# 16-wide attentions with another order of query halves, and a norm whose powers and products are split between GpSimd and VectorE

## The reference, cut to what matters

```python
Q = split_heads(x @ Wq.T)        # 16 heads, 16 wide
K = split_heads(x @ Wk.T)
V = split_heads(x @ Wv.T)
scores = jnp.einsum('bhqd,bhkd->bhqk', Q, K) / jnp.sqrt(jnp.float32(HEAD_DIM))
causal = jnp.tril(jnp.ones((s, s), dtype=bool))
scores = jnp.where(causal, scores, jnp.float32(-jnp.inf))
attn = jax.nn.softmax(scores, axis=-1)
```

```python
nrm = jnp.linalg.norm(x, axis=-1, keepdims=True) * d ** (-0.5)
h = norm_scale * x / (nrm + EPS) * split_scale      # EPS = 1e-08
```

## Time and profile before

| | |
|---|---|
| time, 3 runs | 3187.84, 3194.51, 3197.19 us; median 3194.51 us |
| the profiled execution | 3189.21 us; its span 3187.5 us |
| mean granted TensorE clock of the span | 0.983 |
| busy: TensorE, VectorE, ScalarE, GpSimd | 2986.1, 1373.9, 1113.0, 588.8 us |

### The profile page before, as it was taken

The page is one execution under the profiler, slowest core; times in us unless marked ns, Lnnn a source line. Parts: engine busy times, 40 slices in busy tenths (PEclk is TensorE's granted clock), DMA queues, the critical chain, the costliest instruction groups (busy, mean ns, idle before and its releaser), DMA issues. The chain is left out here.

```text
span 3187.5 us, 40136 instructions
## 1 busy us (share of the span) xinstructions
PE 2986.1 (94%) x15070; PEld 1793.0 (56%) x15070; DVE 1373.9 (43%) x3111; ACT 1113.0 (35%) x1988; POOL 588.8 (18%) x821
## 2 busy tenths in 40 slices
PE   7989999889999999999999999999999999989756
PEld 3443455644465555556666666656776778644413
DVE  6758424576144114212233333333333332277497
ACT  3635414446132113111433433323333332236432
POOL 2020012120002222222000000023333331120163
PEclk9999999999999999999999999999999999999989
DMA  3021000030102331322100000000000000120131
GB/s 84 27 58 50 25 23 26 7 72 6 48 11 76 88 101 44 89 84 81 42 11 10 14 12 22 1 31 12 15 16 11 16 32 12 37 62 22 59 125 60
DMA packets 70507, 129.25 MB, mean 41 GB/s; under 512 B 15918, under 2 KB 43920, under 8 KB 70048
## 3 DMA queue, kind: packets, MB, share of 16 engines
q1 hardware_dynamic: 68396, 125.12, 13.2%
q10 hardware_dynamic: 1920, 1.57, 0.4%
HBM read 99.55 MB, written 1.54 MB: 32 GB/s over the span
## 5 line engine op out<-in xcount | busy, mean ns | idle before, releaser
L186 POOL TENSOR_SCALAR shift<-mv 128x1 f32<-128x1 f32 (+1 forms) x98 | 21.8, 223 | 1465.9 <-DVE scale L171 1465.7
L2289 DVE TENSOR_TENSOR L1f_inner<-L1f_ps_up,L1f_gate 128x512 f32<-128x512 f32 x96 | 66.4, 691 | 362.3 <-PE L1f_ps_up L2188 362.2
L1537 ACT ACTIVATE L2b_tanh<-L2b_ps_scores,L2b_inverse 128x512 f32<-128x512 f32 x192 | 110.6, 579 | 303.4 <-PE L2b_ps_scores L1495 303.4
L2270 ACT ACTIVATE L1f_gate<-L1f_ps_gate 128x512 f32<-128x512 f32 x96 | 57.4, 597 | 399.7 <-PE L1f_ps_gate L2169 399.7
L1134 ACT ACTIVATE L0f_weights<-L0f_ps_scores 128x1024 f32<-128x1024 f32 (+1 forms) x192 | 149.8, 812 | 111.1 <-PE L0f_ps_scores L966 84.1
L2152 POOL TENSOR_TENSOR L1f_inner<-L1f_inner,L1f_weight 128x512 f32<-128x512 f32 x96 | 119.2, 1266 | 365.8 <-DMA L1f_weight<-combine 350.6
L1504 PEld LDWEIGHTS L2b_ps_out<-L2b_v,L2b_weights 128*128 128x128 f32 x1152 | 141.3, 193 | 33.7 <-issue 28.4
L1942 ACT ACTIVATE L2a_probs<-L2a_ps_scores,L2a_negmax 128x512 f32<-128x512 f32 (+7 forms) x128 | 95.1, 743 | 172.3 <-DVE L2a_negmax L1976 172.3
L1495 PE MATMUL L2b_ps_scores<-L2b_q,L2b_k 128*128 128x512 f32 (+3 forms) x384 | 147.4, 487 | 1.0 <-DVE L2b_q L1597 0.8
L1504 PE MATMUL L2b_ps_out<-L2b_v,L2b_weights 128*128 128x129 f32 x1152 | 143.7, 277 | 2.9 <-POOL L2b_weights L1413 2.8
L1839 PE MATMUL L2a_ps_scores<-L2a_k,L2a_q 128*128 128x512 f32 (+3 forms) x384 | 145.2, 487 | 0.0
(11 more groups left out here) (639 smaller groups left out, 6274.1 us busy)
## 6 DMA issues: line engine op xcount, KB each, us to landing
L1f_w<-in_L1f_w SPq DMA_DIRECT2D x32, 384.0 KB, 3.8
L1f_weight<-combine SPq DMA_DIRECT2D x32, 384.0 KB, 4.5
L1f_weight<-combine SPq DMA_DIRECT2D x32, 256.0 KB, 4.7
scan_spread_b<-bc SPq DMA_DIRECT2D x16, 512.0 KB, 4.5
scan_spread_c<-bc SPq DMA_DIRECT2D x16, 512.0 KB, 3.9
L0f_qs<-L0f_part SPq DMA_DIRECT2D x96, 64.0 KB, 2.6
experts_early<-in_L1f_w SPq DMA_DIRECT2D x16, 384.0 KB, 3.6
L2a_early<-in_L2a_w SPq DMA_DIRECT2D x16, 384.0 KB, 3.1
```

The source lines that it names most:

```text
L1537: nc.scalar.activation(tanhs[u % 3][:, at:], ps_scores[u % 3][:, at:], ACT.Tanh, scale=inverse[e][:, NT + kt:NT + kt + 1]).then_inc(capped, 1)
```

## The change

In the attentions the second unit is now (quad 1, half 0) in place of (quad 0, half 1), so units 0 and 1 are both of half 0. The start written by hand has p6, v1 and p7 in other places: p7 now stands ahead of t0. The transfers of the stacked queries and keys follow the new order of units. r0, r2, r3, y4, y6 and f0 stand at other slots. In the norm GpSimd keeps the two powers, and three VectorE operations (`find_shift`) make the sum with the product by 1e-8, the reciprocal, and the shift; the constant -1 for the third power is gone. The number of idle-filling matmuls ahead of each of the last three turns is 4 in place of 8.

```diff
-QUAD_UNITS = [(0, 0), (0, 1), (1, 1), (2, 1), (3, 1), (1, 0), (2, 0), (3, 0)]
+QUAD_UNITS = [(0, 0), (1, 0), (0, 1), (1, 1), (2, 1), (3, 1), (2, 0), (3, 0)]
...
-    order = ("p0 p1 p2 p3 v0 p4 m0 m1 m2 p5 m3 m4 m5 v1 m6 m7 m8 p6 m9 m10 v2 m11 m12 m13 t0 p7 "
+    order = ("p0 p1 p2 p3 v0 p4 m0 m1 m2 p5 m3 m4 m5 p6 m6 m7 m8 v1 m9 m10 p7 m11 v2 m12 m13 t0 "
              "m14 m15 m16 v3 m17 m18 m19").split()
...
-    then(3, 1, "r2")
-    then(5, 1, "r3")
-    then(6, 1, "r0")
+    then(2, 1, "r0")
+    then(4, 1, "r2")
+    then(6, 1, "r3")
     if factor:
-        then(6, 0, "f0")
+        then(7, 0, "f0")
     else:
-        then(6, 0, "y4")
-        then(7, 0, "y6")
+        then(7, 0, "y4")
+        then(7, 1, "y6")
...
-            stack(0, 1)
+            stack(1, 0)
             sp.dma_start(ks[SPLIT:WITH_MAX, :, :, :].rearrange("i a h t -> i (a h t)"), core.ones_rows
                          ).then_inc(ones_in, 16)
             for u in range(NU):
+                if u < 2:
+                    stack(u, 1)
+                elif u < QUADS:
+                    stack(u, 1)
+                    stack(u, 0)
                 place_max(u)
-                if u < QUADS - 1:
-                    stack(u + 1, 0)
-                    stack(u + 1, 1)
...
-        pool.wait_ge(done, n + 1)
-        pool.tensor_scalar(scale, scale, 1e-8, None, ALU.mult).then_inc(done, 1)
-        pool.wait_ge(done, n + 3)
-        pool.tensor_tensor(scale, scale, shift, ALU.add).then_inc(done, 1)
-        pool.wait_ge(done, n + 4)
-        pool.tensor_tensor(scale, scale, inverse, ALU.pow).then_inc(done, 1)
-        pool.wait_ge(done, n + 5)
-        pool.tensor_tensor(shift, mean, scale, ALU.mult).then_inc(self.turned_mean, 1)
-        pool.wait_ge(self.turned_mean, g + 1)
-        pool.tensor_scalar(shift, shift, -1.0, None, ALU.mult).then_inc(self.shifted, 1)
+
+    def find_shift(self, dve, g):
+
+        if self.kind != "norm":
+            return
+        core, part = self.core, self.tiles(g)
+        scale, shift = core.scale[:, part], core.shift[:, part]
+        dve.wait_ge(self.scaled, 2 * (g + 1))
+        dve.scalar_tensor_tensor(scale, scale, 1e-8, shift, ALU.mult, ALU.add).then_inc(self.inverted, 1)
+        dve.wait_ge(self.inverted, 2 * g + 1)
+        dve.reciprocal(scale, scale).then_inc(self.inverted, 1)
+        dve.wait_ge(self.inverted, 2 * g + 2)
+        dve.scalar_tensor_tensor(shift, core.mv[:, part, 0], -1.0, scale, ALU.mult, ALU.mult).then_inc(self.shifted, 1)
...
-                keep_busy(core, ps_out[0][:], 8 if following.kind == "norm" else 4)
+                keep_busy(core, ps_out[0][:], 4)
...
                 following.find_spread(nc.vector, t)
+                if t:
+                    following.find_shift(nc.vector, t - 1)
                 if t >= 4:
                     following.keep_dve(nc.vector, t - 4, free_bank(t - 4))
+            following.find_shift(nc.vector, NT - 1)
```

More of the change, by code:

```diff
@@ L41, in __init__ @@
         self.zeros = sb("zeros", [P, HALF], BF16)
-        self.powers = sb("powers", [P, 3 * NT])
+        self.powers = sb("powers", [P, 2 * NT])
         self.ident = sb("ident", [P, P])
@@ L120, in open @@
         self.x_added, self.measured, self.spread = st.sem("next_x_added"), st.sem("next_measured"), st.sem("next_spread")
-        self.scaled, self.turned_mean = st.sem("next_scaled"), st.sem("next_turned_mean")
+        self.scaled, self.inverted = st.sem("next_scaled"), st.sem("next_inverted")
         self.shifted, self.rows_act = st.sem("next_shifted"), st.sem("next_rows_act")
@@ L181, in find_scale @@
         size = part.stop - part.start
-        inverse_root, root, inverse = (core.powers[:, n * NT:n * NT + size] for n in range(3))
-        n = (5 if self.kind == "norm" else 2) * g
+        inverse_root, root = (core.powers[:, n * NT:n * NT + size] for n in range(2))
+        n = 2 * g
         if self.kind != "norm":
@@ L306, in _ @@
             nc.vector.memset(core.powers[:, NT:2 * NT], 0.5).then_inc(powers_set, 1)
-            nc.vector.memset(core.powers[:, 2 * NT:3 * NT], -1.0).then_inc(powers_set, 1)
             nc.vector.memset(rows[:], 1.0).then_inc(rows_set, 1)
@@ L349, in _ @@
             nc.gpsimd.memset(core.zeros[:], 0.0).then_inc(ones_set, 1)
-            pool.wait_ge(powers_set, 3)
+            pool.wait_ge(powers_set, 2)
             for q in range(4):
@@ L1256, in keep_turned @@
             def keep_turned(n):
-                if n == 2:
+                if n == 0:
                     dve.wait_ge(projected, len(PROJECTIONS))
```

## The result

| | before | after |
|---|---|---|
| median of 13 runs | 3190.74 us | 3168.25 us |
| range | 3177.09 to 3197.19 | 3153.76 to 3177.74, and one of 12891.03 apart |
| profiled execution (span, mean clock) | 3189.21 (3187.5, 0.983) | 3164.59 (3162.9, 0.990) |

What follows compares the result with a forecast made beforehand. VectorE was taken to set the pace in the openings, GpSimd in the norm. Gains of 16.6 + 6.0 + 1.9 + 5.9 = 30.4 us off 3189.2 gave 3158.8; with half the spread added, 3161 us, range 3144 to 3180.

Steps and rivals of the forecast that it cites:

- The openings: s0 to n0 of the four 16-wide attentions: 20.5 us each at clock 1.00, winning 16.6 us in all.
- the fewer pieces: Openings: VectorE does pieces 20 to 48 instead of 20 to 51 before n0; 1.8 us a stage, 7.2 as bound.
- The clock stayed: Openings: clock taken as 1.00; the rival that it still falls cost 5 to 14 us, chance 0.18.
- Ahead of s0: Starts of the four attention stages: p7 ahead of t0 removes waits there; 6.0 us gained in sum, 0 from below.
- Net 0.9 in three stages: L0a and both L0f starts: waits of 1.24 us at t0 go, less masked pieces' cost of 0.4 less 0.1.
- In L3a … 3.3: L3a's start: 2.08 us wait goes, half-clock projection of 3.50 becomes 1.98, less 0.3; 3.3 us gained.
- Behind the openings: End of a layer, within n0 to n7: 1.9 us gained in L0a and L3a, the rest unchanged.
- s88: Slot late in L0a: its 0.93 us wait for maxima goes as y4 moves on, likewise in L3a.
- only moved: Rival: work moves behind n0, n0 to n7 grows by up to 2.9 us a stage, 12 us back; chance 0.11.
- The norm: Norm with less GpSimd work: rounds of 1.9, then 2.6 us; 5.9 us gained, bounds 4.5 and 6.8.
- the shared interface: Norm: GpSimd's powers might hold VectorE's two-SBUF-input operations; 16 would cost 9.1 us, total 8.9 higher; nothing was charged.
- the slow queue: Rival: SyncE's 24 stacking transfers delay unit 2's maxima at s16; at twice today's price 3205 us; chance 0.03.

Runs made afterwards that it cites:

- unit 2 from s0: The changed kernel with the third unit's 27 pieces spread from slot 0 on instead of slot 3; executed once, 3165.74 us.

## Why the prediction was right, and where it was not

**The openings: right, 15.4 for 16.6.** They take 20.8 us where I had 20.5. Only the second L0f stage, at 1.00 in both profiles, prices the fewer pieces alone: 1.56 us for 1.8. What the other three won beyond that, 9.1 us, hangs on the clock and on the waits for keys in L0a and L3a. The clock stayed, which I held likeliest: 41 of the 44 openings of kernels with the changed order (without "unit 2 from s0") are at 1.00 and 20.7 to 20.9 us, of eight with the old order one is at 1.00. Each of the three that fell has a part_max of the second unit stretched by GpSimd inside it, to 2.25 to 3.62 us, where it takes 1.00 to 1.30 in the 41; behind it TensorE waited 1.30 to 2.68 us. The rule of the Trainium skill, TensorE: Matmul & The Clock Gate, section "A second HAM failure mode: psum-queue depth-cycling", would have both orders swing: TensorE goes through the same three banks in both, yet one keeps the clock.

**Ahead of s0: this step failed, 1.5 for 6.0.** "Net 0.9 in three stages. In L3a … 3.3." Three things were wrong. The wait at t0 fell from 1.24 us to 0.19 or nothing, but 0.28 and 0.26 came back at the next two pieces, also in L0a; in L3a it fell from 2.08 to 0.38, and 0.96 and 0.26 came back. A part is the longer part_max. In the first L0f stage, where it takes 2.92 us, m0 to s0 is 0.3 us longer than in the second, where it takes 1.85; in L3a, where it takes 2.67, it is 0.8 longer than in the runs in which it takes 1.0. The masked pieces cost 0.5 us of TensorE, not 0.3. And in L3a I booked 1.5 us for a half-clock p7 as saved; the low clock came at p5 instead. With GpSimd's reads out of the way the old start is as short or shorter, so p7 bought nothing there.

**Behind the openings: failed too, +3.1 for -1.9.** s88 no longer waits, as I said. But the rival "only moved" was partly true: 1.44 us of new waits at n0, m52 and t2 in every stage. I had argued against it with a mean over 112 us (VectorE busy for 75.8); the place where VectorE is late, the third unit's part_max and what follows it, is 3 us long.

**The norm: right, 6.6 for 5.9.** The small operations step by 0.19 to 0.20 us, not 0.21, and the rounds are 1.72 and 2.31, not 1.9 and 2.6. (With 0.3 us for each small operation my own sum gives 3.7 us as the low bound, not 4.5; the range had room for it.) I weighed the shared interface here and took nothing, which held: seven of the eight L207 stand beside a power and take 0.16. It acted in the starts instead, and in three openings of the experiments, where I never asked which VectorE steps read two SBUF tiles beside GpSimd.

**The rest.** 4.2 us of the profiled gain have no changed instruction behind them. So the changed places give 20.4 us, two thirds of my 30.4, and the total, which lay in the range, looked nearer than its terms; that was luck. Of the rivals, the slow queue stayed away: no slot waits for its maxima in after. (At twice today's price it would have cost 12 us a stage by my own numbers, not 11, and 16 held operations in the norm 9.1, not 8.9.) What makes the clock fall in an opening stays open. The runs show two things after which it can fall, pieces packed between s0 and s3, and a stall of over a microsecond right behind. The first doesn't do it always: the second L0f stage of before kept 1.00 with the same instructions.

## What to carry to other kernels

Before moving work between engines, list the VectorE instructions on the path that read two SBUF tiles, and look what GpSimd reads at that time: a step of 0.17 us can last to the end of GpSimd's instruction, and a wait for VectorE's own progress on GpSimd mends it, if the work put off doesn't meet the next such step. A forecast of a saved wait needs the next thing that is late, in a window of a few microseconds, never the mean of a stage. Where single executions differ by 10 to 20 us, size an edit of 2 us by the lengths of its stages in the trace and leave the median to the whole.

## What the runs showed of the hardware

- A VectorE step of 128x16 with both inputs in SBUF can last to the end of GpSimd's addition or subtraction of two tiles: operations of 1.04, 1.16 and 4.52 us gave steps of up to 1.03, 1.18 and 2.79 us. Beside 120 writes of 0.52 us it took 0.17.
- Beside GpSimd's scaling of 128x256 by a number a row (1.2 us), which also reads, such a step took 0.17 us mostly and never over 0.53.
- Beside GpSimd's power on one number a row (0.55 us), a two-input step was not held (0.16 us, seven times). Why not, in either case, no run here shows.
- 3.9 us of stretched steps in a stage went with 9.9 us more of it: TensorE waited behind them, and its clock was 0.86 and then 0.96.
- With no instruction changed, a stretch of 2.0 ms took between 1987.7 and 2008.4 us in 14 executions, at mean granted clocks of 0.997 to 0.986.
